# A DLRM tower in fp32: one more item of the third cross layer is computed from split operands, its difference made by VectorE

## What is computed

```
for i in range(3):                       # x0: [B, 32, 16], h: x0, then [B, 64, 16]
    z = (x0[:, :, None, :] * h[:, None, :, :]).reshape(B, F * G, E)
    y = relu(einsum('oc,bce->boe', W[i], z) + b[i])     # 128 outputs
    x_keep, h = (y[:, :64], y[:, 64:]) if i < 2 else (y, y)
z = sum over e of concat(x_keep)         # [B, 256]
h = relu(concat([z, dense]) @ W_top1 + b_top1)
h = relu(h @ W_top2 + b_top2);  out = h @ W_top3
```

## Time and profile before

| | us |
|---|---|
| median of three runs | 1074.82 (1073.98 to 1075.13) |
| the profiled execution | 1078.64 |
| its span | 1076.8 |
| PE busy | 997.7 |
| DVE busy | 824.0 |
| POOL busy | 821.6 |
| ACT busy | 475.1 |

### The profile page before, as it was taken

One profiled execution on the slowest core, in us unless ns is written; L12 is line 12 of the kernel. 1 busy time (PEld: TensorE's weight loads), 2 busy tenths in 40 slices (PEclk: granted clock), 3 DMA queues, 4 the chain that ended last, 5 costly groups with the idle time before them and its releaser, 6 DMA issues.

```text
span 1076.8 us, 11324 instructions
## 1 busy us (share of the span) xinstructions
PE 997.7 (93%) x3089; PEld 569.0 (53%) x3089; DVE 824.0 (77%) x750; ACT 475.1 (44%) x595; POOL 821.6 (76%) x524
## 2 busy tenths in 40 slices
PE   2177899999999999999999999999999999999988
PEld 1033455555555555555555555555555555555555
DVE  4245788888778788887778777987778877888882
ACT  2132444355435444445435544444435454444453
POOL 7565779798897989797988989797979955666640
PEclk8588999999999999999999999999999999999999
DMA  7079989789987989799987988798987988889200
GB/s 156 5 167 204 204 191 204 156 192 205 200 189 159 206 193 191 168 206 201 198 187 162 206 186 188 175 204 192 203 179 170 202 197 186 188 187 215 66 1 0
DMA packets 49013, 185.45 MB, mean 172 GB/s; under 512 B 17571, under 2 KB 22179, under 8 KB 28389
## 3 DMA queue, kind: packets, MB, share of 16 engines
q1 hardware_dynamic: 40804, 183.15, 77.3%
q0 software_dynamic: 8192, 2.11, 1.8%
HBM read 182.06 MB, written 3.15 MB: 172 GB/s over the span
## 4 chain that ended last, share of the span: by engine, by line
PE 41%; POOL 24%; issue 17%; DVE 8%; ACT 4%; another core or an unknown queue 3%; DMA 1%; SPq 1%; POOLq 0%; DVEq 0%; ACTq 0%
PE y L616 26%; POOL low L499 16%; PE y L624 8%; POOL looked_up L489 8%; PE y L639 5%; DVE unsplit L1069 2%; DVE prod L1069 2%; DMA spread<-in_L_rec_W 1%; PE xT L588 1%; DVE acc_kept L1100 1%; POOL tail_parts L507 1%; ACT h L814 1%; DMA shifted<-xcols 0%; DVE low L1077 0%
## 5 line engine op out<-in xcount | busy, mean ns | idle before, releaser
L499 POOL TENSOR_TENSOR low<-unsplit,high 128x1024 fp32r<-128x1024 f32 x221 | 530.9, 2414 | 130.7 <-ACT high L828 126.2
L616 PE MATMUL y<-prod,w1T 128*128 128x512 f32 x1024 | 478.7, 596 | 7.2 <-issue 5.0
L1069 DVE TENSOR_TENSOR prod<-spread,h 128x1024 f32<-128x1024 f32 x288 | 346.5, 1213 | 72.3 <-PE y L616 59.6
L828 ACT CAST high<-unsplit 128x1024 fp32r<-128x1024 f32 x224 | 234.5, 1048 | 310.3 <-DVE unsplit L1069 300.5
L1069 DVE TENSOR_TENSOR unsplit<-spread,h 128x1024 f32<-128x1024 f32 x224 | 271.7, 1213 | 102.2 <-ACT h L814 96.8
L489 POOL DMA_INDIRECT looked_up<-in_tbl,ids_now x256 | 248.2, 970 | 65.4 <-issue 56.4
L616 PEld LDWEIGHTS y<-prod,w1T 128*128 128x128 f32 x1024 | 192.3, 191 | 169.6 <-issue 148.2
L624 PE MATMUL y<-high,w2T_high 128*128 128x512 f32 x448 | 225.3, 503 | 1.5 <-ACT high L828 1.5
L639 PE MATMUL y<-low,w2T_high 128*128 128x512 f32 x448 | 203.7, 535 | 12.4 <-POOL low L499 12.1
L624 PE MATMUL y<-high,w2T_low 128*128 128x512 f32 x448 | 177.0, 395 | 0.0
L814 ACT ACTIVATE h<-y,bias 64x512 f32<-64x512 f32 x128 | 83.4, 652 | 163.1 <-PE y L616 138.2
(11 more groups left out here) (115 smaller groups left out, 407.9 us busy)
## 6 DMA issues: line engine op xcount, KB each, us to landing
spread<-xcols SPq DMA_DIRECT2D x128, 1024.0 KB, 9.3
shifted<-xcols SPq DMA_DIRECT2D x124, 256.0 KB
shifted_tail<-xcols SPq DMA_DIRECT2D x124, 64.0 KB
looked_up<-in_tbl,ids_now POOLq DMA_INDIRECT x256
xcols<-xrows SPq DMA_DIRECT2D x32, 96.0 KB
spread<-in_L_rec_W SPq DMA_DIRECT2D x3, 512.0 KB, 4.9
spread<-in_L_rec_W SPq DMA_DIRECT2D x1, 1024.0 KB
wt<-in_W_top SPq DMA_DIRECT2D x2, 512.0 KB, 9.9
```

Source lines behind the costliest of these rows:

```text
L499: pool.tensor_tensor(low[kind][r][:, :, :], unsplit[kind][r][:, :, :], high[kind][r][:, :, :].bitcast(F32), ALU.subtract).then_inc(s_low[k ...
L616: last = pe.matmul(y[:, :], w, z[:, c, :], start=(n == 0 and c == 0), stop=(item in (LAST0, LAST1) and c == ITEM - 1))
L828: act.copy(high[kind][r][:, :, :], unsplit[kind][r][:, :, :]).then_inc(s_high[kind], 1)
L1069: dve.tensor_tensor(z, x[:, ITEM * n:ITEM * (n + 1), :], b[:, :].unsqueeze(1).to_broadcast([P, ITEM, COLS]), ALU.mult).then_inc(s_made[kin ...
```

## The change

Item (2, 6) becomes an item of kind BY_DVE in the slots 1 to 31, and one of kind BY_POOL in the last slot, 32. The whole weight `w2T_whole` and its copy at the start are gone.

```
-WHOLE2 = (2, 6)
+SPLIT2_BY_DVE = [(2, 6)]
 LAST_BY_DVE = [(2, 2), (2, 5), (2, 7)]
...
 def kind_of(item, last):
-    if item[0] < 2 or item == WHOLE2:
+    if item[0] < 2:
         return WHOLE
-    return BY_DVE if last and item in LAST_BY_DVE else BY_POOL
+    return BY_DVE if item in (LAST_BY_DVE if last else SPLIT2_BY_DVE) else BY_POOL
...
-        w2T_whole = sb("w2T_whole", [P, ITEM, P])
...
-                        w = w2T_whole[:, c, :] if layer == 2 else (w0T, w1T)[layer][:, ITEM * n + c, :]
+                        w = (w0T, w1T)[layer][:, ITEM * n + c, :]
...
-                    if WHOLE2[1] // (GROUP // ITEM) == n - 2 - GROUPS:
-                        of = ITEM * WHOLE2[1] % GROUP
-                        dve.tensor_copy(w2T_whole[:, :, :], source[:, of:of + ITEM, :])
```

## The result

The changed kernel takes 1080.92 us (median of 4 runs, 1080.01 to 1081.15) against 1074.43 for the kernel before: a ratio of 1.006, 95% interval 1.0048 to 1.0073. It is slower by 0.6%, where 1061.2 us, 1.3% faster, was forecast.

A forecast was written before the change was run, and what follows sets the result against it. PE was taken as the bound, plus about 2.5 us per four slots from POOL and DVE. PE's 9.9 us plus 10.7 from lockouts less 7.0 for POOL's delay gave 13.6 us gained: 1061.2 us, range 1056 to 1072.

The forecast's parts named there:

- What PE saves: On PE, splitting (2, 6) takes 1.40 us instead of 1.72: 0.32 us saved in each of 31 slots, 9.9 us in all.
- ACT's rounding at nothing: On ACT, one more rounding of 1.05 us per slot, hidden by 3.22 us idle before h1: cost 0.
- DVE's time at nothing: On DVE, the new 1.21 us subtraction per slot, hidden with 2.3 us left until PE would feel it: cost 0.
- POOL held by 0.85 us in each slot: DVE's new two-SBUF-input subtraction delays a POOL lookup 0.85 us per slot; PE loses 1.17 us in six slots, 7.0 us.
- the lockout is gone: In slot 16 and its like, DVE's addition no longer waits behind POOL's two subtractions: 1.78 us gained six times, 10.7 us.
- the signs of being wrong: In the changed profile: additions or copy over 4 us, DVE's new subtraction 3 us or more, PE waiting at slot starts.
- the 0.03 us: In slot 16 before the change, DVE's addition starts at 557.40, POOL's first subtraction at 557.43.
- the walk: Step-by-step timing of a block, slots 14 to 17, under the change: slot 18 starts 1.93 us earlier.
- POOL's cycle of 28.1 us: POOL from slot 15's first subtraction to slot 16's: 27.27 us plus 0.85, still under PE's 28.99, so not too slow.
- The slower rival: POOL passes DVE's new subtraction, so PE waits for (1, 0), losing 1.8 us per slot; 1076 to 1100 us; chance 0.07.
- The rival that the lockout comes back at another place: DVE's copy in slot 17 or new subtraction gets caught behind POOL, giving back 1.78 us per block; 1066.5 to 1071.9; chance 0.22.
- The rival that lookups aren't held: DVE's new subtraction doesn't delay POOL's lookups, so gains total 18.7 us: 1056.1 us; chance 0.12.

## Why the prediction was wrong

**What PE saves: right.** Slots that PE bounds last 29.01 to 29.03 us, 28.99 was said.

**ACT's rounding at nothing: right,** by the run that has it alone in the kernel before, and by the one with the operand in PSUM, which keeps it. **DVE's time at nothing: right,** by the two runs that differ only in it.

**POOL held by 0.85 us in each slot: right in slot 14 and 16, wrong in slots 15 and 17.** It was 0.8, 0, 0.8 and 0.4 us. In slot 15 the subtraction starts just behind a lookup's start and holds nobody. I had shown bounds of 0.15 and 0.85 us and then used one value for all slots, although whether a lookup is held depends on which instruction of POOL is running, and that differs from slot to slot.

**The step that failed: "POOL has been held once more in slot 15 and starts at 559.13. The addition is now 1.2 us ahead of it ... the lockout is gone".** It wasn't gone in any of the six blocks: 10.7 us that weren't gained. Additions of over 4 us are also the first of the signs of being wrong that I had named. Two errors made it. One is the missing delay in slot 15. The other is that I let the addition follow the start of the slot. It follows h1, which is released by (1, 7), and (1, 7) stands ahead of the place where PE saves its 0.32 us: the addition comes 555.90 - 554.14 = 1.76 us into slot 16, where it came 1.45 us into it. When PE is pinned by POOL's first subtraction in slot 15, both the addition (531.09 to 555.90, 24.81 us, and 557.40 - 532.59 = 24.81 us before) and POOL's next first subtraction (27.29 us, 27.27 before) follow from that one point. Nothing that the change does behind it moves one against the other, and the 0.03 us became 0.05. By the walk's own numbers either error alone would have left the addition ahead, by 0.9 or by 0.35 us; with both it stayed where it was. The run with the operand in PSUM shows the second error by itself: nothing is held there, PE has its saving, and the addition still takes 5.3 us in all six blocks.

**A wait that I worked out and didn't charge.** The walk puts POOL's (2, 7) of slot 14 at 522.70 + 0.85 = 523.55, to 525.9, and PE wanting it at 525.13: a wait of 0.8 us at the end of slot 14, which the next wait in slot 15 would absorb. In slot 16, where nothing absorbs it, I asked only whether POOL's cycle of 28.1 us fits in 28.99. A cycle that fits on average says nothing of an instruction that has no slack: before, POOL's subtraction for (2, 7) in slot 16 ended just when PE came to it. There 0.8 us of holding and 0.32 us of saving make a wait of 1.10 us, six times. With the operand in PSUM, where nothing is held, it is 0.3 us.

**The slower rival** named the right place, the new subtraction against POOL, but a wait of DVE; the longest there are 2.5 us, and in the slots from 3 to 31 PE waits for a product of DVE only behind the six locked-out additions (0.6 us each, 0.3 before). What made the kernel slower is the other side of the same meeting. The rival that the lockout comes back at another place was closest in kind, at 1071.9 us: it came back at the same place. The rival that lookups aren't held gave 1056.1 us; the two runs in which the subtraction holds none took 1072.7 and 1073.2, since that rival, too, let the lockout go. The holding of lookups that the Trainium skill's page (SBUF — State Buffer, "Who interferes with whom") infers not to happen is measured: 8.2 us hang on whether the second operand lies in SBUF.

**Where the 9.9 us went.** Without either meeting they show as 4.4 us (3.2 by the ratios), or 3.6 with lookups moved (1051.5 against 1055.1). The 31 slots give 0.30 us each, 9.2 us and not 9.9, if nothing waits (29.31 against 29.01 us). The two profiles with lookups moved put the rest mainly in two places: some 3 us in the slots 7, 11, 15, 19 and 23, to POOL's lateness, which 29.3 us of PE covered and 29.0 us don't, and some 2 us in the slots 1 to 3. Both are read from the profiles, not shown by a run.

## What to carry to other kernels

Where two engines exclude each other on a resource, walk each meeting through by itself, with the instruction that is running on the other side at that moment; a mean delay per round predicts neither the holding nor the lockout. Before work is shortened on the engine that bounds, ask which releases stand ahead of the saved place: they don't move, and the chains that hang on them keep their offsets, the bad ones too. A lockout can be worth far more than any saving near it: moving one 0.7 us addition by one product brought 17.5 us.

## What the runs showed of the hardware

A DVE instruction with two SBUF inputs waited for two of POOL's subtractions back to back (5.29 us for 0.68), where its row starts 0.05 us ahead of the first and the DVE product before it ends 0.03 us behind that one's start. In slot 14 of the kernel before the addition took 1.91 us and got in between the two, and the second took 2.84 us for 2.38. The two cases differ in when ACT's rounding for the second subtraction ended: 0.2 us before the first subtraction did in slot 14, 1.2 us before it in slot 16. That this decides is not shown. A copy of 128 x 512 in fp32, 0.42 us alone, is locked out as well (5.04 us).

A table lookup on POOL is held when it starts under such a DVE instruction (1.77 us for 0.96 near its start, 1.33 us when 0.5 us of it were left), and wasn't when it started 0.18 us before it (547.68 and 547.86, 0.96 us) or 0.14 us before its end (548.95, 0.96 us). With the operand in PSUM the subtraction holds none.
